# Attention of a macaron block: scores by two fp32r parts and two heads side by side

## The reference

```
x = x + 0.5 * ffn(layernorm(x))
x = x + attention(layernorm(x))
x = x + 0.5 * ffn(layernorm(x))        # same weights as the first

ffn(x)       : h = silu(x @ w_gate) * (x @ w_up)            # hidden 1024
               keep the 2 largest |h| of each 4, others 0;  h @ w_down
attention(x) : q = rope(x @ Wq + bq), 32 heads of 8;  k = rope(x @ Wk + bk), v = x @ Wv + bv, 8 heads
               softmax(q k^T / sqrt(8), causal) v;  @ Wo + bo
```

## Time and profile before

| | |
|---|---|
| median of 3 runs | 912.97 us |
| profiled execution: time, span | 914.1 us, 912.4 us |
| mean granted TensorE clock | 0.956 of 2.4 GHz |
| busy: PE, DVE, ACT, POOL | 815.6, 749.0, 497.9, 252.4 us |
| first matmul of attention, its last PV | 250.7, 710.0 us |
| first exponential of attention | 276.9 us |

### The profile page before, as it was taken

How to read it: one execution, slowest core, us unless ns; L and a number is a source line. 1 busy time by engine, 2 the same in 40 slices (tenths; PEclk the granted TensorE clock), 3 DMA queues, 4 the chain that set the end, 5 groups by cost and what they waited for, 6 DMA issues and landing times. The chain is left out here.

```text
span 912.4 us, 15884 instructions
## 1 busy us (share of the span) xinstructions
PE 815.6 (89%) x5248; PEld 479.6 (53%) x5248; DVE 749.0 (82%) x1929; ACT 497.9 (55%) x972; POOL 252.4 (28%) x320
## 2 busy tenths in 40 slices
PE   4999996588589999999999999999998679999986
PEld 3787875576423333333333333333332468778776
DVE  4999989777598888988988988888880475999986
ACT  6444443123207777777777777777778223443441
POOL 1152344336521221222221222221222000443250
PEclk9999999789869999999999999999999789999997
DMA  7000000226923211222211222211210210000001
GB/s 267 1 1 1 1 1 0 95 84 184 284 72 70 64 36 48 73 73 74 70 40 38 73 73 73 73 51 29 69 41 8 69 51 1 0 25 1 24 0 47
DMA packets 38977, 52.11 MB, mean 57 GB/s; under 512 B 3568, under 2 KB 29040, under 8 KB 37488
## 3 DMA queue, kind: packets, MB, share of 16 engines
q1 hardware_dynamic: 38896, 51.10, 19.7%
HBM read 22.78 MB, written 16.25 MB: 43 GB/s over the span
## 5 line engine op out<-in xcount | busy, mean ns | idle before, releaser
L1106 ACT ACTIVATE att_probs<-att_s_ps 128x512 f32<-128x512 f32 (+1 forms) x640 | 306.8, 555 | 99.4 <-PE att_s_ps L1012 97.3
L1069 DVE CUSTOM_DVE_ANT_0 att_scratch<-att_m_ps,att_causal 128x512 bf16<-128x512 f32 (+3 forms) x512 | 234.2, 486 | 31.1 <-PE att_m_ps L997 28.3
L997 PE MATMUL att_m_ps<-mk,mq 128*128 128x512 bf16 (+3 forms) x768 | 241.7, 336 | 19.6 <-PEq L519 11.1
L1012 PE MATMUL att_s_ps<-sq,sk 128*128 128x512 bf16 (+3 forms) x768 | 218.8, 329 | 5.9 <-ACT att_probs L1106 4.1
L1072 DVE TENSOR_REDUCE att_maxima<-att_m_ps 128x1 f32<-128x512 f32 x256 | 175.9, 687 | 13.1 <-PE att_m_ps L997 11.8
L1029 PE MATMUL att_o_ps<-att_probs,att_vs 128*32 128x512 f32 (+3 forms) x1536 | 156.8, 496 | 1.4 <-POOL att_probs L1175 1.1
L1175 POOL TENSOR_SCALAR_AFFINE_SELECT att_probs<-att_probs 128x512 f32<-128x512 f32 x128 | 79.0, 634 | 269.4 <-ACT att_probs L1106 269.4
L997 PEld LDWEIGHTS att_m_ps<-mk,mq 128*128 128x128 bf16 x768 | 73.0, 98 | 116.2 <-DVE att_maxima L1069 46.5
L1012 PEld LDWEIGHTS att_s_ps<-sq,sk 128*128 128x128 bf16 x768 | 71.2, 97 | 119.1 <-ACT att_probs L1106 80.5
L465 POOL TENSOR_TENSOR ffn_hs_lo<-ffn_hs,ffn_hs_hi 128x512 fp32r<-128x512 f32 x56 | 90.7, 1644 | 131.4 <-ACT ffn_hs_hi L314 131.4
L268 PE MATMUL ffn_y_ps<-wd_hi,ffn_hs_hi 128*128 128x256 f32 x256 | 74.9, 292 | 19.1 <-DVE x L400 18.9
(11 more groups left out here) (121 smaller groups left out, 1221.0 us busy)
## 6 DMA issues: line engine op xcount, KB each, us to landing
q_rows<-qkv_parts SPq DMA_DIRECT2D x24, 384.0 KB, 3.6
mq<-q_rows SPq DMA_DIRECT2D x16, 576.0 KB
sq<-mq SPq DMA_DIRECT2D x16, 576.0 KB
k_rows<-qkv_parts SPq DMA_DIRECT2D x12, 192.0 KB, 2.9
mk<-k_rows SPq DMA_DIRECT2D x16, 144.0 KB
sk<-mk SPq DMA_DIRECT2D x16, 144.0 KB
sum_tiles<-att_sums SPq DMA_DIRECT2D x128, 18.0 KB
tile_sums<-sum_tiles SPq DMA_DIRECT2D x16, 144.0 KB, 2.2
```

The source lines that it names most:

```text
L997: pe.matmul(m_ps[bank][:, :n], mq[e][:, h, t * P:(t + 1) * P], mk[e][:, kc * N:kc * N + n], start=True, stop=True).then_inc(m_done, 1)
L1012: last = pe.matmul(s_ps[(u * QPK + h) % S_BANKS][:, at:at + w], sk[e][:, kb * P:(kb + 1) * P], sq[e][:, h, qc * N + q0:qc * N + q0 + w], s ...
L1069: dve.tensor_tensor_reduce(out=scratch[bank][:, :n], in0=m_ps[bank][:, :n], in1=causal[:, N - n:], scale=1.0, scalar=LOWEST, op0=ALU.add, ...
L1106: act.activation(probs[u % len(probs)][:, h, SPAN[u]], s_ps[(u * QPK + h) % S_BANKS][:, SPAN[u]], ACT.Exp, scale=SCALE).then_inc(exp_done, 1)
```

## The change

- **Projections.** The rotated q and k are split into two fp32r parts instead of three bf16 parts. ACT takes the high part; the low part is taken by DVE (units 0 and 1) or POOL (unit 2). The middle part, `rest` and the zero fills on POOL go. Each part is stored twice, as fp32: four rows per dimension, 32 rows in all, and with the two rows of the shift 34. The two further rows of `mq` and `mk` (zeros) and of `sk` (-1), are filled by twelve small DMAs.
- **Two heads side by side.** The first head of a pair stands in partitions 0 to 33, the second in 64 to 97, so that their matmuls use different row groups of TensorE. A group has 24 pairs of matmuls for M and 24 for S.
- **M.** A unit of M is a tile of 128 queries with one block of keys, for two heads (two banks) or, where it is at most 256 wide, for all four; there are 20 units a group, two per step, and two places of two banks. The causal mask of a diagonal block is added by TensorE: a constant `future` (-1e30 above the diagonal) multiplied by two selections, 64 columns each, for each head. DVE takes one TENSOR_REDUCE per unit.
- **S.** Still three banks, which now also take the turned shifts (two a group, in the same ring). A pair waits until its second bank is free.
- **Order.** A step is: pair 0 of S, M, pair 1 of S, M, PV, and after steps 2 and 9 the turn of a shift.
- **Splitting the maxima.** The maxima are kept twice; DVE joins only those of the second half; POOL makes both parts of the shift.
- The helper that put a wait on an instruction of its own (`wait_apart`) goes everywhere.

The core of the diff:

```diff
             def lo_part(c, u):
-                dve.wait_ge(mid_ready, c * UNITS + u + 1)
-                dve.wait_ge(stored[u][2], 16 * c)
-                dve.tensor_tensor(parts[:, u, 2, :], rest[:, u, :], parts[:, u, 1, :], ALU.subtract).then_inc(lo_ready, 1)
+                dve.wait_ge(hi_ready, c * UNITS + u + 1)
+                dve.wait_ge(stored[u][1], 16 * c)
+                dve.tensor_tensor(parts[:, u, 1, :], turned[:, u, :], parts[:, u, 0, :].bitcast(F32), ALU.subtract)\
+                   .then_inc(lo_ready[u], 1)
...
-                if not first:
-                    lo_part(c - 1, 2)
...
             def add_turned(c, u):
                 pool.wait_ge(by_ready, c * UNITS + u + 1)
+                if u < UNITS - 1:
+                    pool.wait_ge(lo_ready[u], c)
                 pool.tensor_tensor(turned[:, u, :], by_cos[:, u, :], by_sin[:, u, :], ALU.add).then_inc(turned_ready, 1)
-            def leave_rest(c, u):
-                if u == 0:
-                    pool.wait_ge(lo_ready, c * UNITS)
+            def lo_part(c, u):
                 pool.wait_ge(hi_ready, c * UNITS + u + 1)
-                pool.tensor_tensor(rest[:, u, :], turned[:, u, :], parts[:, u, 0, :], ALU.subtract).then_inc(rest_ready, 1)
+                pool.wait_ge(stored[u][1], 16 * c)
+                pool.tensor_tensor(parts[:, u, 1, :], turned[:, u, :], parts[:, u, 0, :].bitcast(F32), ALU.subtract)\
+                    .then_inc(lo_ready[u], 1)
...
+                    for part in range(2):
+                        rows = (q_rows[u * P:(u + 1) * P, 2 * part:2 * part + 2, tokens] if u < QM
+                                else k_rows[:, part::2, tokens])
+                        src = parts[:rows.shape[0], u, part, :].bitcast(F32)
+                        if part:
+                            sp.wait_ge(lo_ready[u], c + 1)
+                        else:
+                            sp.wait_ge(hi_ready, c * UNITS + u + 1)
+                        sp.dma_start(rows, src[:, None, :].to_broadcast([rows.shape[0], 2, N]))\
                           .then_inc(stored[u][part], 16)
             FIRST_BATCH = group_rows.T // N
...
+    def load_m(self, sp, g):
+        r, e = g // 2, g % 2
         tokens = slice(e * self.T, (e + 1) * self.T)
+        for w in range(2):
+            sp.dma_start(self.mq[e][self.rows(w)].bitcast(F32), self.q_groups[r, w, :, :, tokens]).then_inc(self.m_loaded[e], 16)
+            sp.dma_start(self.mk[e][self.rows(w)].bitcast(F32), self.k_groups[r, :, tokens]).then_inc(self.m_loaded[e], 16)
+    def copy_s(self, sp, g, copied):
+        e = g % 2
+        for w in range(2):
+            sp.dma_start(self.sq[e][self.rows(w)].bitcast(F32), self.mq[e][self.rows(w)].bitcast(F32)).then_inc(copied[e], 16)
+            sp.dma_start(self.sk[e][self.rows(w)].bitcast(F32), self.mk[e][self.rows(w)].bitcast(F32)).then_inc(copied[e], 16)
...
+    M_UNITS = []
+    for t in range(KB):
+        for kc in range(t // TPC + 1):
+            n = min(N, (t + 1) * P - kc * N)
+            M_UNITS += [(t, kc, n, (0, 1))] if 2 * n <= N else [(t, kc, n, (0,)), (t, kc, n, (1,))]
...
+    M_SLOTS = 2
+    PROBS = 5
+    TURN_AT = (2, SU - 1)
+    assert MU % M_SLOTS == 0 and MU == 2 * SU and MU_HALF == 2 * (1 + M_LEAD)
...
+    RING = QPK * SU + QC
+    assert RING % S_BANKS == 0
+    place, placed = {}, 0
+    for g in range(-1, GROUPS):
+        for u in range(SU):
+            v_g, v_u = (g, u + AHEAD) if u + AHEAD < SU else (g + 1, u + AHEAD - SU)
+            if 0 <= v_g < GROUPS and (g >= 0 or u + AHEAD >= SU):
+                for h in range(QPK):
+                    place[v_g, v_u, h] = placed
+                    placed += 1
+            if u in TURN_AT and g + 1 < GROUPS:
+                place[g + 1, "turn", TURN_AT.index(u)] = placed
+                placed += 1
...
+            def m_unit(g, j):
+                e, i = g % 2, g * MU + j
+                t, kc, n, pairs = M_UNITS[j]
+                diagonal = kc == t // TPC
+                if j == 0:
+                    pe.wait_ge(m_loaded[e], 16 * LOADS * (g // 2 + 1))
+                if i >= M_SLOTS:
+                    pe.wait_ge(m_taken, i - M_SLOTS + 1)
+                out = m_ps[i % M_SLOTS]
+                for k, a in enumerate(pairs):
+                    for w in range(2):
+                        rows = group_rows.rows(w, 0, ROWS + SHIFT)
+                        last = pe.matmul(out[:, w, k * n:(k + 1) * n], mq[e][rows, a, t * P:(t + 1) * P],
+                                         mk[e][rows, kc * N:kc * N + n], start=True, stop=not diagonal, skip_group_check=True)
+                    if diagonal:
+                        for pick, at in ((stay, (k + 1) * n - P), (turn, (k + 1) * n - P // 2)):
+                            for w in range(2):
+                                half = slice(64 * w, 64 * w + 64)
+                                last = pe.matmul(out[:, w, at:at + P // 2], pick[half, :], future[half, :],
+                                                 start=False, stop=pick is turn, skip_group_check=True)
+                last.then_inc(m_done, 1)
...
+            def s_pair(g, u, a):
...
+                second = place[g, u, 2 * a + 1]
+                if second >= S_BANKS:
+                    pe.wait_ge(s_taken, second - S_BANKS + 1)
+                for n, (kb, q0, width, at) in enumerate(pieces):
+                    for w in range(2):
+                        rows = group_rows.rows(w, 0, ROWS + SHIFT)
+                        last = pe.matmul(s_ps[place[g, u, 2 * a + w] % S_BANKS][:, at:at + width],
+                                         sk[e][rows, kb * P:(kb + 1) * P],
+                                         sq[e][rows, a, qc * N + q0:qc * N + q0 + width], start=True, stop=True)
+                        if n == len(pieces) - 1:
+                            last.then_inc(s_done, 1)
...
+            def maxima_of(g, u, slot):
+                late = u + M_LEAD >= SU
+                m_g, j = (g + 2, 2 * (u + M_LEAD - SU) + slot) if late else (g + 1, 2 * (u + M_LEAD) + slot)
+                if m_g < GROUPS:
+                    m_unit(m_g, j)
+            def step(g, u):
+                s_g, s_u = ahead(g, u)
+                for a in range(2):
+                    if s_g < GROUPS:
+                        s_pair(s_g, s_u, a)
+                    maxima_of(g, u, a)
+                if g >= 0:
+                    value_unit(g, u)
+                if u in TURN_AT and g + 1 < GROUPS:
+                    turn_shift(g + 1, TURN_AT.index(u))
...
+                    i = g * MU + j
+                    scores, found = m_ps[i % M_SLOTS], maxima[g % 2][:, t, kc, :]
+                    dve.wait_ge(m_done, i + 1)
+                    if len(pairs) == 2:
+                        dve.tensor_reduce(found.rearrange("p (a w) -> p w a", w=2),
+                                          scores[:, :, :2 * n].rearrange("p w (a n) -> p w a n", a=2),
+                                          mybir.AxisListType.X, ALU.max).then_inc(m_taken, 1)
+                    else:
+                        dve.tensor_reduce(found[:, 2 * pairs[0]:2 * pairs[0] + 2], scores[:, :, :n],
+                                          mybir.AxisListType.X, ALU.max).then_inc(m_taken, 1)
...
+            def split_maxima(g, qc):
+                found = maxima[g % 2]
+                tiles = slice(qc * TPC, (qc + 1) * TPC)
+                if qc:
+                    pool.wait_ge(joined_ready, g + 1)
+                else:
+                    pool.wait_ge(m_taken, g * MU + MU_HALF)
+                whole = top[:] if qc else found[:, tiles, 0, :]
+                if g:
+                    pool.wait_ge(s_taken, place[g - 1, "turn", qc] + 1)
+                pool.tensor_copy(shift[qc][:, :, :, 0], whole).then_inc(split_step, 1)
+                pool.wait_ge(split_step, QC * g + qc + 1)
+                pool.tensor_tensor(shift[qc][:, :, :, 1], whole, shift[qc][:, :, :, 0], ALU.subtract).then_inc(shift_ready, 1)
```

More of the change, by code:

```diff
@@ new lines, in fill @@
+    def fill(self, sp):
+        W = self.CONSTANTS
+        sp.wait_ge(self.constant_set, 2)
+        for w in range(2):
+            extra = self.rows(w, self.ROWS, self.ROWS + self.SHIFT)
+            for e in range(2):
+                for tile, value in ((self.mq[e][extra].rearrange("p a t -> p (a t)"), 0), (self.mk[e][extra], 0), (self.sk[e][extra], 1)):
+                    pieces = tile.shape[1] // W
+                    sp.dma_start(tile.bitcast(F32).rearrange("p (n c) -> p n c", c=W),
+                                 self.constant[:, value][:, None, :].to_broadcast([self.SHIFT, pieces, W])).then_inc(self.filled, 16)
@@ L815, in attention_phase @@
     GROUPS = B * KVH
-    QPK = group_rows.QPK
+    QPK = 4
     KB = T // P
@@ L841, in attention_phase @@
     MU = len(M_UNITS)
-    MU_HALF = TPC * QPK
-    halves = [sorted(half, key=lambda unit: -unit[3]) for half in (M_UNITS[:MU_HALF], M_UNITS[MU_HALF:])]
```

(46 more changed lines are left out.)

540 lines of the change are left out of this document (196 added, 344 removed).

## The result

The changed kernel takes **1128.5 us** (median of 4 runs, 1121.9 to 1162.5), the kernel before beside it 912.9. The ratio is 1.233, 95% interval 1.227 to 1.239: slower by 23%. The slowest of the four runs, 1162.5 us at a mean clock of 0.687 where the other three have 0.716 to 0.730, is left out of the ratio. I had forecast slower, 945 us, with 975 as the upper end; the time is far outside. The profiled execution took 1121.9 us, its span is 1119.9.

The account below looks back on a forecast made before the run. PE's order of work was taken to set the 27.16 us group, above a loop of exponential, S, PV, S; +41 (periods), +1 (attention start) and -9 (projections) made +33, forecasting 945 us, range 914 to 975.

Parts of the forecast that it names:

- rival C: TensorE clock in attention falls to 1.2 GHz in a quarter of the time: +4 us a group, 1005 us; chance 0.07.
- Part 1: Steady attention group: period 29.9 us (27.9 to 31.5) against 27.16, giving +41 us over fifteen periods.
- (a): Steady group's loop of exponential, S, PV, S: ten steps without any M take 23.1 us.
- (d): fp32r in S, a pair instead of one bf16 matmul: 1.0 us a group (0 to 1.8).
- (e): Second shift's turn moves from step 8 to 9, so S waits for it at step 1: 1.8 us (1.4 to 2.2).
- (b): Second M unit of each step stands in the loop: 12 pair slots at 0.235, 2.8 us a group.
- (c): Mask matmuls on TensorE: 8 of 16 fall on units in the loop, 1.2 us a group (0.5 to 2.4).
- Part 2: Start of attention: PE waits for 20 small POOL operations before its first maximum; net +1 us (-2 to +4).
- Part 3: Projections: POOL zero fills go, shorter DVE waits, fewer operations before the last store; together -9 us (-5 to -11).
- rival A: Loop has unseen slack and the shift lands in time: 25.8 to 26.5 us a group, 890 us; chance 0.25.
- B: A pair's two heads don't run side by side: 35 us a group, about 1025 us; chance 0.05.
- D: No change: steady loss of 0.5 us a group cancels the 9 us gained; chance 0.05.

Follow-up runs that it names:

- experiment 8: The kernel before, with S and M contracting only 37 rows (half the parts of q and k left out): 1256.1 us, ratio 1.375.
- 64-row kernel: The changed kernel with each head contracting 64 rows instead of 34, the added rows zero: 967.2 us, ratio 1.060.
- experiment 7: The 64-row kernel with both maxima units of a step between its two pairs of heads, instead of one after each: 921.8 us, ratio 1.011.
- experiment 6: The 64-row kernel without the causal mask matmuls on TensorE: 949.2 us, ratio 1.040.
- experiment 5: The 64-row kernel with the second shift turned at step 8 instead of step 9: 935.0 us, ratio 1.022.
- Experiment 11: The 64-row kernel with both maxima units between the pairs, second turn at step 8, and mask tiles built in the projections: 900.2 us, ratio 0.985.
- experiment 3: The changed kernel with two extra side-by-side pairs of 34-row matmuls on PE in each step: 981.7 to 1036.7 us, no ratio.
- experiment 10: The changed kernel, still 34 rows a head, with both maxima units between the pairs and second turn at step 8: 984.2 us (958.5 to 1005.8).
- experiments 4 and 8: Experiment 4: the kernel before, with S and M contracting 74 rows instead of 128: 916.0 us, ratio 1.003; experiment 8 has its own line.

## Why the prediction was wrong

**The step that failed is rival C, the clock:** "If it falls to 1.2 GHz in a quarter of the time, the PE terms of those steps (1.6 us each) double: +4 us a group, 1005", at a chance of 0.07. The price of a step held: ten times 1.6 is 16 us, and a group at half speed is 15.0 us longer (44.75 - 29.71). What failed is how much of the time it holds, and the chance; the sum of the forecast took every term at full clock. Half speed holds in most of eleven of the fifteen periods, about 164 us or 11 a period instead of 4, and in the whole stretch before them, which is 13 us longer. I read the earlier trace rows as busy time alone, 5.25 of 6 us for full and 3.19 of 5 for partly half speed, and set 24 of 30 us beside them. But all those rows are of a kernel whose matmuls cover 128 rows (S, M and PV), and the diff itself said that those of S and M would now cover 34 + 34. Nor had I asked whether the state would last: at half speed PE is busy 42.93 of 44.75 us and stays at half all the same, from group to group. The Trainium skill (TensorE: Matmul & The Clock Gate, Part 1) says that the gate is set by "how busy the PE has been recently"; the row of experiment 8, busy 49.56 of 49.56 us at 0.50, shows that busy time in the profile is not enough to judge that by. The runs show that rows and waiting both count; what exactly the chip measures stays open. The last of the prediction's own signs of being wrong, "if the clock falls", is the one that came.

**Part 1 without the clock was right in its form, and in its sum partly by luck.** Predicted 29.9 us a period, measured 29.71 at clock 1.00 in the 64-row kernel, PE at "some 24" and measured 24.4. But (a) to (d) were 0.5 us too low together and (e) 0.7 too high, and within the four the terms were off in both directions. By terms:
- (a) and the form of the loop: the full step with masks is 2.93 us; by my terms 2.46 + 0.235 + 0.15 + 0.1, that is 2.95. The wait for ACT before the second pair is 0.49 (predicted 0.3 to 0.5).
- (b) and (c), the unit in the loop with its masks: 2.8 + 1.2 predicted, 2.26 given back by experiment 7, which also lengthened the wait for the shift from 1.18 to 1.44 us: 2.5. All masks cost 0.69 (experiment 6), not 1.2. A pair takes 0.33 to 0.34 us of PE (502.51 to 502.84), not 0.235. That is dearer, and yet the two terms together cost less; which part is hidden, no run shows.
- (a) to (d) together: without the shift's wait the period is 28.59, where they gave 28.1. (d) was not tested alone.
- (e) 1.8 predicted; PE idles 1.18 and the period loses 1.12 (experiment 5). The weight load waits longer, 1.86 us on average in the changed kernel; that is not the price.
- DVE: 20.5 predicted, 22.2 to 22.3 measured; a reduction of 1024 elements follows the last by 1.23, not 1.13. In the fifteen periods of the 64-row kernel PE never waited for it.

**Part 2**: +1 predicted. The mask tiles hold the first maximum up by 4.0 us; before it came 0.2 after its block began. Experiment 11 moves them: 5 us less in the medians (3 to 3.8 expected), 3.9 in the wait of PE. **Part 3**: -9 predicted, the block of attention begins 10.3 us earlier. The first normalisation takes 1.38 us instead of 5.50. Together -6.45, predicted -8.

**The ends of the range** do not follow from the parts: added up as they stand they give 911 and 977, not 914 and 975. And rival A's own 890 lies below 898, though more than half of A is said to lie above that.

With its clock held the forecast would have stood: the profiled 64-row run took 965.9 us with periods of 462.1 in sum; with the 436 to 440 of full clock the estimate for the run is 940 to 944, where I had said 945. The +41 for the periods was 36 to 40.

**The rivals.** A (faster, 890): not for the kernel as changed, but the slack it speaks of exists in another order, with 64 rows: 900 us in experiment 11. B (heads not side by side): a pair's two matmuls run in 0.50 us where one over all rows takes 0.38 to 0.40, and the pair holds up what follows for 0.33, between the 0.235 of side by side and the 0.47 of one after the other. B in full is excluded, and the heads do overlap, but not freely. D (no change) is excluded.

## What to carry to other kernels

When a change packs small contractions side by side or trims rows, read the granted clock of the new kernel before anything else, and try zero rows up to the full height of each head's row group (64 here): they cost no column, only bytes of fill, and here they are worth 161 us. Before such a change, compare rows contracted and not only busy time with the stretches in which the clock was full. Remove waits of PE as well: taking away the one at step 1 gave 32 us, of which 17 are the wait itself and most of the rest is clock. Then look for work that stands in a loop between two engines and move it to where the engine waits anyway: 2.3 us a group here, for two exchanged lines.

## What the hardware showed that I had not expected

- The same 202 matmuls a group ran at 1.2 GHz when those of S and M had 37 rows, without a gap, and at 2.4 GHz with 74 or 128, the columns being equal (49.56 and 27.16 us a group). Rows that hold zeros count: 30 of them a head brought the mean clock from 0.73 to 0.92.
- A program that has both levels of the clock can differ from run to run: 1122 to 1163 us (the changed kernel), 982 to 1037 (experiment 3), 959 to 1006 (experiment 10), and within one execution between 26.2 and 41.5 us for the same group of work (experiment 10). Where attention stays at one level (experiments 4 and 8) the runs agree within 0.4%.
- Two matmuls in different row groups take 0.33 us at 512 columns until the next can start, against 0.23 for one over all rows; at half clock 0.59.
